# Node passes in rank order, with a pipeline of its own on each engine

## What is computed

```python
x = _layernorm(x + _L0_gnn_ref(x, edge_index, 12500, L0_gnn_W), axis=-1)
x = _layernorm(x + _L1_gnn_ref(x, src, dst, L1_gnn_W_n, L1_gnn_a_src, L1_gnn_a_dst, ...), axis=-1)
x = _layernorm(x + _L2_gnn_ref(x, edge_index, L2_gnn_W, L2_gnn_b), axis=-1)
x = _layernorm(x + _L3_gnn_ref(x, edge_index, edge_weight, L3_gnn_We1, ...), axis=-1)
```

## Time and profile before

| | us |
|---|---|
| median of 3 runs | 9929.16 |
| lowest, highest | 9925.69, 9943.68 |
| profiled execution, its own time | 9940.12 |
| its span | 9938.3 |

### The profile page before, as it was taken

One profiled execution on the slowest core, in us unless ns is written; L12 is line 12 of the kernel. 1 busy time (PEld: TensorE's weight loads), 2 busy tenths in 40 slices (PEclk: granted clock), 3 DMA queues, 4 the chain that ended last, 5 costly groups with the idle time before them and its releaser, 6 DMA issues. The chain is left out here.

```text
span 9938.3 us, 113228 instructions
## 1 busy us (share of the span) xinstructions
PE 5334.2 (54%) x29001; PEld 4290.1 (43%) x29001; DVE 5628.4 (57%) x12677; ACT 1827.5 (18%) x6201; POOL 6156.5 (62%) x6454
## 2 busy tenths in 40 slices
PE   0255555555366666666664454454435666666653
PEld 0233444444255555555553333333334555555532
DVE  2467777775477777777332222222256777777745
ACT  0000000001155555555320000000021111111121
POOL 0777777771577777776007777777636777777700
PEclk9866666667688988888885555555567777777766
DMA  4222222221444444444111111111234444444411
GB/s 101 71 54 54 53 54 54 54 52 50 114 120 118 121 120 119 119 119 104 47 48 53 53 53 53 53 53 53 64 111 117 119 119 119 119 118 119 118 37 35
DMA packets 932390, 822.38 MB, mean 83 GB/s; under 512 B 370017, under 2 KB 776073, under 8 KB 931435
## 3 DMA queue, kind: packets, MB, share of 16 engines
q0 software_dynamic: 231344, 523.28, 19.6%
q1 hardware_dynamic: 700480, 292.47, 11.6%
HBM read 735.15 MB, written 79.95 MB: 82 GB/s over the span
## 5 line engine op out<-in xcount | busy, mean ns | idle before, releaser
L682 POOL DMA_INDIRECT rows_h<-t_d,idx x3126 | 2991.8, 957 | 1290.1 <-issue 920.2
L811 PE MATMUL pn_h<-S_h,rows_h 128*128 128x128 f32 x9378 | 1817.7, 339 | 702.5 <-DVE lo_h L1004 459.1
L422 POOL DMA_INDIRECT rows_sum<-t_d,idx x1563 | 1478.2, 946 | 992.1 <-ACTq L359 515.9
L811 PEld LDWEIGHTS pn_h<-S_h,rows_h 128*128 128x128 f32 x9378 | 1559.3, 234 | 1019.8 <-issue 976.9
L422 POOL DMA_INDIRECT rows_mlp<-t_d,idx x1563 | 1482.2, 948 | 486.7 <-issue 476.4
L461 PE MATMUL pn_sum<-S_sum,rows_sum 128*128 128x128 f32 x3126 | 806.8, 440 | 970.2 <-DMA rows_sum<-t_d,idx 970.2
L461 PEld LDWEIGHTS pn_sum<-S_sum,rows_sum 128*128 128x128 f32 x3126 | 694.5, 327 | 1236.9 <-issue 1236.6
L720 ACT ACTIVATE rows_h<-rows_h,wc_h 128x64 f32<-128x64 f32 x4688 | 1133.8, 333 | 9.8
L529 DVE TENSOR_TENSOR acc<-acc,pn_sum 128x512 f32 x391 | 269.1, 688 | 1441.6 <-PE pn_sum L461 1441.4
L446 PE MATMUL pre_mlp<-dw_mlp,ST_mlp 128*128 128x128 f32 x3126 | 585.2, 346 | 764.8 <-DVE ST_mlp L56 764.1
L446 PEld LDWEIGHTS pre_mlp<-dw_mlp,ST_mlp 128*128 128x128 f32 x3126 | 502.6, 244 | 841.0 <-issue 789.2
(11 more groups left out here) (262 smaller groups left out, 7359.8 us busy)
## 6 DMA issues: line engine op xcount, KB each, us to landing
dw_mlp<-bd_d SPq DMA_DIRECT2D x1563, 64.0 KB
rows_h<-t_d,idx POOLq DMA_INDIRECT x3126, 2.5
n_xi<-x_d SPq DMA_DIRECT2D x56, 448.0 KB, 6.3
lrb_h<-lrrow_d SPq DMA_DIRECT2D x98, 256.0 KB
lrb_mlp<-lrrow_d SPq DMA_DIRECT2D x98, 256.0 KB, 3.5
dw_h<-sd_d SPq DMA_DIRECT2D x1563, 3.0 KB
rows_sum<-t_d,idx POOLq DMA_INDIRECT x1563
rows_mlp<-t_d,idx POOLq DMA_INDIRECT x1563
```

The costliest lines, as they stand in the source:

```text
L422: e.indirect_dma_start(rows[:, g % NR, j, :], None, table, bass.IndirectOffsetOnAxis(ap=idx[:, b, t:t + 1].bitcast(I32), axis=0)).then_inc ...
L682: e.indirect_dma_start(rows[:, g % NR, j, :], None, table, bass.IndirectOffsetOnAxis(ap=idx[:, b16, t:t + 1].bitcast(I32), axis=0)).then_i ...
L811: last = e.matmul(pn[g % 2][:, k, bass.ds(r0, P)], rows[:, g % NR, j, k * P:(k + 1) * P], S[:, g % NS, j, :], start=False, stop=last_tile)
```

## The change

Only node pass 0 still takes node order in. It scatters the normalized rows by rank to `xp_d`: 136 columns, which are x, the target scores in 6, the degree and the node number. The table `t1_d` gets one more column, the rank of its node, and the edge pass of layer 1 copies it from the gathered rows over `idx`, batch by batch. So later tables and gathers are in rank order, and `node1`, `node2` and `node3` read the accumulator `big` as it lies. `big[:, 0]` holds x between passes; GpSimd clears `big[:, 1]` during node passes 1 and 2, in the place of a clearing at the start of the edge passes. `node3` sends each tile of the result to its nodes with an indirect DMA. The one-hot matrix, the windows, the copy and the turn of the window, and x_d go from passes 1 to 3; the scatter goes from pass 2; passes 1 and 2 store plainly.

Each node function is written out as straight-line programs over 25 units of four tiles (the last has two), one for each engine, with a semaphore for each hand-over. Centring and scaling of a layer norm become one ScalarE activation for each tile (scale and bias by partition). In passes 2 and 3, which need gelu and square root, units go in chunks of 6, 6, 6, 4, 2 and 1, and the square roots of a chunk are taken together. Pass 3 multiplies We2 and Wu1's lower half once ahead of the loop (`V`) and so does one 512-column product less for each unit. Biases are added in passes 2 and 3 by a matmul over one row.

In the edge pass of layer 1, local ranks and `dw` come in blocks of 8 tiles, not 16; `dw` reads 24 of the 544 bytes of a row of `xp_d`, and `ex` waits for its own block, not for all 32 tiles of the batch. In the setup, 100 clearing DMAs of `bd_d` and one of `sd_d` become two small ones, and the store of `x_d` goes.

```diff
-W0, W1 = F + 1, H * DH + H
...
+W0, W1, XR = F + 1, H * DH + H + 1, F + 8
...
-                for k in range(DRANKS // P):
-                    e.dma_start(bd_d[k * P:(k + 1) * P, :], zero[:, 0:F]).then_inc(s_st, 16)
-                e.dma_start(sd_d.rearrange("(p k) h -> p (k h)", p=P),
-                            zero[:, 0:DRANKS // P * 3 * H // 2].bitcast(BF16)).then_inc(s_st, 16)
+                for table, w in ((bd_d, F), (xp_d, XR)):
+                    e.dma_start(table[NP:DRANKS, :].rearrange("(p k) f -> p (k f)", p=P), zero[:, 0:2 * w]).then_inc(s_st, 16)
...
-                e.dma_start(x_d.rearrange("(t p) f -> p t f", p=P), xs[:, :, 0:F]).then_inc(s_o, 16)
...
-            e.memset(acc[:, :, :], 0.0)
...
-                        m = (b * TB + k) // NB
-                        many = min(NB, have - k)
+                    for k in range(0, have, LB):
+                        m = (b * TB + k) // LB
+                        many = min(LB, have - k)
                         if m >= 2:
-                            e.wait_ge(s_st, (m - 1) * NB // 4)
-                        e.dma_start(lrb[:, m % 2, :], d["lrrow"][m:m + 1, :].broadcast_to([P, EB])).then_inc(s_lrb[m % 2], 16)
+                            e.wait_ge(s_st, (m - 1) * LB // 4)
+                        e.dma_start(lrb[:, m % 2, :], d["lrrow"].rearrange("(o b) e -> o (b e)", o=1)[:, m * LB * P:(m + 1) * LB * P]
...
-                        r0 = load_values(nc, SP, regs[BASE:BASE + 1, m * NB:m * NB + many], N)
+                        r0 = load_values(nc, SP, regs[BASE:BASE + 1, m * LB:m * LB + many], N)
                         for t in range(many):
-                            e.dma_start(dw[:, b % 2, k + t, :], d["sd"][bass.ds(r0[t], P), :]).then_inc(s_dw[b % 2], 16)
+                            e.dma_start(dw[:, b % 2, k + t, :], d["xp"][bass.ds(r0[t], P), F:F + 3 * H // 2]).then_inc(s_dw[m % 4], 16)
...
-                if g % GB == 0:
-                    if b > 0:
-                        e.wait_ge(s_chain, at(b - 1, "score"))
-                    e.wait_ge(s_dw[b % 2], 16 * sum(fetched[k] for k in range(b % 2, b + 1, 2)))
+                if g % GB == 0 and b > 0:
+                    e.wait_ge(s_chain, at(b - 1, "score"))
+                m = 4 * g // LB
+                if 4 * g % LB == 0:
+                    e.wait_ge(s_dw[m % 4], 16 * sum(min(LB, TILES - k * LB) for k in range(m % 4, m + 1, 4)))
...
+                        at0 = b * TB
+                        e.tensor_copy(idx[:, :, :].rearrange("p b t -> p (b t)")[:, at0:at0 + 4 * ng].bitcast(I32)
+                                      .rearrange("p (g t) -> p g t", t=4), rows[:, u:u + ng, :, W1 - 1])
                         e.wait_ge(s_ex, min(GR, (b + 1) * GB))
```

More of the change, by code:

```diff
@@ L1597, in node_pass @@
[L1597 to L1617 removed]
+            return ctx.enter_context(nc.semaphore(f"n0_{name}"))
@@ L1653, in _ @@
         @block.tensor
         def _(e):
[L1655 to L1663 removed]
+            e.wait_ge(s_w, 64)
+            for h in range(H):
+                for k in range(2):
+                    last = e.matmul(psc[0][:, 0, k * H + h:k * H + h + 1], wnT[:, h, :], a2[:, k, h:h + 1], start=True, stop=True)
@@ new lines, in _, with turn_acc, pick @@
+            last.then_inc(s_v, 1)
+            def turn_acc(u):
+                n = unit(u)[1]
+                e.wait_ge(s_win, u + 1)
+                if u > 0:
+                    e.wait_ge(s_Ar, u)
+                for j in range(n):
+                    last = e.transpose(pa[:, j, :], win[u % 2][:, j, :], ident[:, :])
+                last.then_inc(s_A, 1)
+            def pick(u):
+                n = unit(u)[1]
+                e.wait_ge(s_Ar, u + 1)
+                e.wait_ge(s_Es, u + 1)
+                if u > 0:
+                    e.wait_ge(s_y, u)
+                for j in range(n):
+                    last = e.matmul(pe[:, j, :], Es[u % 2][:, j, :], Ar[u % 2][:, j, :], start=True, stop=True)
+                last.then_inc(s_E, 1)
@@ new lines, in turn, with table @@
+            def turn(u):
+                n = unit(u)[1]
+                e.wait_ge(s_n, u + 1)
+                if u > 0:
+                    e.wait_ge(s_xT, u)
+                for j in range(n):
+                    last = e.transpose(pt[:, j, :], xs[u % 3][:, j, 0:F], ident[:, :])
+                last.then_inc(s_T, 1)
+            def table(u):
+                n = unit(u)[1]
+                e.wait_ge(s_xT, u + 1)
+                if u == 0:
+                    e.wait_ge(s_vs, 1)
+                else:
+                    e.wait_ge(s_tab, u)
+                if u >= 2:
+                    e.wait_ge(s_row, u - 1)
+                for j in range(n):
+                    last = e.matmul(ph[:, j // 2, j % 2, :], xT[u % 2][:, j, :], wn[:, :, :].rearrange("p h d -> p (h d)"),
+                                    start=True, stop=True)
+                last.then_inc(s_H, 1)
+                for j in range(n):
+                    last = e.matmul(psc[u % 2][:, j, :], xT[u % 2][:, j, :], vs[:, :], start=True, stop=True)
+                last.then_inc(s_S, 1)
@@ new lines, in normal, with hide @@
+            def normal(u):
+                t, n = unit(u)
+                e.wait_ge(s_rs, u + 1)
+                for j in range(n):
+                    last = e.activation(big[:, 0, (t + j) * P:(t + j + 1) * P], y[u % 2][:, j, :], ACT.Identity,
+                                        scale=rs[u % 2][:, j, :], bias=nm[u % 2][:, j, :])
+                last.then_inc(s_n, 1)
+            def hide(u):
+                n = unit(u)[1] * P
+                e.wait_ge(s_H, u + 1)
+                if u >= 2:
+                    e.wait_ge(s_O, u - 1)
+                for j in range(2):
+                    last = e.activation(hid[u % 2][:, j, 0:n], ph[u % 2][:, j, 0:n], ACT.Relu, bias=b1[:, j:j + 1])
+                last.then_inc(s_hid, 1)
@@ new lines, in turned @@
+            def turned(u):
+                n = unit(u)[1]
+                e.wait_ge(s_T, u + 1)
+                if u >= 2:
+                    e.wait_ge(s_G, u - 1)
+                e.copy(xT[u % 2][:, 0:n, :], pt[:, 0:n, :]).then_inc(s_xT, 1)
+            positive(0)
+            e.wait_ge(s_dn, 16)
+            e.activation(root[:, :], dn[:, :, 0], ACT.Sqrt, bias=c["ones"][:, 0:1]).then_inc(s_sq, 1)
+            for i in range(UNITS + 3):
+                if i + 1 < UNITS:
+                    positive(i + 1)
+                if 0 <= i - 2 < UNITS:
+                    normal(i - 2)
+                if i < UNITS:
+                    hide(i)
+                if 0 <= i - 2 < UNITS:
+                    turned(i - 2)
+                if 0 <= i - 1 < UNITS:
+                    deviate(i - 1)
```

1255 lines of the change are left out of this document (731 added, 524 removed).

## The result

| | before | after |
|---|---|---|
| median us | 9927.78 (4 runs) | 9308.01 (4 runs) |
| lowest to highest | 9925.69 to 9943.68 | 9301.27 to 9322.9 |
| span of the profiled execution | 9938.3 | 9299.4 |

The ratio is 0.9375, 95% interval 0.9358 to 0.9391: 620 us less, where 828 were forecast. The time lies inside the range.

A forecast was written before the change was run, and what follows sets the result against it. Edge passes were taken as bound by GpSimd's gathers, node passes by hand-overs between engines. Savings of 240 + 130 + 140 + 225 + 65 + 28 = 828 us, and 11 more, off 9940 gave 9100 us, range 8980 to 9340.

The forecast's parts named there:

- The bound before, edge passes by gathers: Edge passes: each lasts as long as its 1,563 gathers, 1.25 us each, 1955 us; no other engine can shorten it.
- Pass 1, -240: Node pass 1: PE sets the pace at 7.3 us a unit, 216 us in all, saving 240 us.
- Pass 3, -225: Node pass 3: 98 new GpSimd scatters start near 95 us and set the end near 238, saving 225 us.
- Setup, -28: Setup: less clearing and no `x_d` store save 28 us.
- edge pass 1, -65: Edge pass 1: `ex` no longer waits for the whole batch; three quarters of 89 us, 65, saved.
- Pass 2, -140: Node pass 2: 4.6 us a unit with PE at full clock, 190 us in all, saving 140 us.
- rival A: Node passes: PE stays at half clock and sets the pace; total near 9350 us, chance 0.12.
- Pass 0, -130: Node pass 0: 6.2 us a unit, 203 us with rank map, start and drain, saving 130 us.
- Rival C: Passes 0 and 3: scatters slow to 1.9 us each beside a busy VectorE; total 9190 us, chance 0.1.
- Rival E: Edge pass 1: strided `dw` reads make SyncE's issues longer, so the kernel gets slower, near 10,300 us; chance 0.04.
- Rival D: Edge pass 1 gives nothing, since `ex` waits for the score chain; total 9165 us, chance 0.2.
- Rival B: Node passes: hand-overs cost 2 us more for each of 100 units, +200; total 9300 us, chance 0.15.

The follow-up runs named there:

- e7: Kernel before, with edge pass 1's expansion waiting only for its own block of 16 tiles: gathers span 1985.7 us for 2043.4, kernel 9866.2 us.
- e8: Changed kernel; pass 2 with products before x transposes, bias on VectorE, idle products in first chunk; four scatter buffers in pass 0: 9071.04 us, ratio 0.9134.
- e10: Changed kernel with four scatter buffers instead of three in node pass 0, nothing else: gap 283.4 us for 340.4, kernel 9248.78 us.
- e3: Changed kernel with node pass 2's bias added by VectorE instead of PE matmuls, on a disturbed chip: gap 246.9 us, control 373.1.

## Why the prediction was right, and where not

- **The bound before, edge passes by gathers: right.** Their spans moved by 4 to 5 us, and what was to be won lay in the node passes, the setup and one wait. For edge pass 1 the 1955 us of 1,563 gathers were a little short: it took 1989.1, against the sign "within 10 us of its gathers". By the windows a gather there kept GpSimd busy for 0.966 us (1509.62/1562), and for 0.943 in the sum pass (1473.96/1563).
- **Pass 1, -240, measured -265: right in the mechanism, with some luck in the price.** I took PE as the pace with 6.3 of 7.3 us; the trace has 6.55 us a unit with PE busy 50.0 of 50 us at clock 1.00. The 5.6 that busy time times mean clock gave was too low; the addition for short pieces and the margin of 1 us covered it.
- **Pass 3, -225, measured -221: GpSimd's sends set its end, as forecast; that the start fitted to 0.5 us is luck.** The first send was forecast at 95 us from the start; it came at 9147.51 - 9052 = 95.5:

```profile
9147.51 1.02 POOL L1998 DMA_INDIRECT out<-n_z,gout  x1 [102.84 <-ACT n_z L2097]
...
9288.82 0.98 POOL L1998 DMA_INDIRECT out<-n_z,gout  x1 [0.30 <-DMA out<-n_z,gout]
```

GpSimd waited 118.9 us in all for the results, 102.84 of them before the first send, and the sends took 141.3 us, for 134. In that start PE was the pace, not VectorE as forecast; it had no idle time in a unit of the first chunk, at full clock:

```profile
9068.16 0.60 PE L2018 MATMUL n_pt<-ident,big 128*128 128x128 f32 x4
...
9069.56 1.12 PE L2031 MATMUL n_pu<-n_dg,n_v 1*128 1x512 f32 x2
9070.61 1.12 PE L2033 MATMUL n_pu<-n_xT,n_wu 128*128 128x512 f32 x2
...
9073.71 0.60 PE L2018 MATMUL n_pt<-ident,big 128*128 128x128 f32 x4
```

That is 5.55 us (9068.16 to 9073.71) for PE's 3.6 of the forecast, and it fell on the 5.5 that I had for the unit. The two chunks ahead of the first send took about 79 us for 63, against a start and boundaries that were shorter; and the forecast's own terms, 14, 30, 33 and two boundaries, come to 85 and not 95 if a boundary is the 4 us of pass 2. In the other runs on undisturbed chips the first send came 2 us earlier to 14 us later.
- **Setup, -28, measured -28.6, and edge pass 1, -65, measured -54: right.** The three quarters that I took were about the size; e7 shows the wait as the only cause. (2.0 us in each of the pass's 49 batches are 98 us, not the 89 of the forecast.)
- **Pass 2, -140, measured +24: wrong, and this is the step that failed.** "3.4 a unit, and with two bias matmuls about 3.2 at full clock" scaled PE's busy time by the mean granted clock of the window, 0.64. But that mean runs over the idle time too, and the busy time lay more at full clock than the idle time. The products of L1505 before ran nearly all at full clock (45.6 us for 392, 0.116 each); of the 113 us in which PE was busy, 67 lay at full clock and 46 at half. At full clock all of it is then 67 + 46/2 = 90 us, an estimate, and without L1481 some 67, 2.7 a unit and not 2.2. The bias rows I took at 0.76 us each before scaling, both together 1.0 at full clock; but a float32 matmul stands in the trace as two instructions, and one bias row of 512 columns is both of them. PE's busy time in the unit above is 9.97 us at half clock, so about 5.0 at full, for the 3.2 of the forecast; 2.1 of them are bias. Second, I took full clock for granted there, though rival A had the other price. Rival A came true in this pass alone ("if PE stays at 0.5 in a node pass" was among the signs of being wrong), and with 9.97 us of PE a unit, not its 6.5, since its price for half clock rested on the same scaling. Third, I read ScalarE's and VectorE's programs for their sums, not for their order beside PE's; the 3.5 us of waiting in each unit were in the order of the three programs and could have been read there.
- With the order turned and the bias off PE, e8 runs at 4.58 us a unit and a gap of 186 us: the pace of 4.6 that the forecast had, and about the 190 us. The size was reachable, not reached; the changed kernel with its two bias matmuls would not have had that pace even at full clock, by the 5.0 estimated above.
- **Pass 0, -130, measured -81: a term of the sum mis-sized.** Pace 6.2 was forecast; 196.5 us over 25 units is 7.9. The scatters themselves were cheap, 0.969 us, below both rows that I had. What was missing is the time for which a buffer is held: filled at step i+2, scattered after step i+4, and landed 2.4 us behind. I had counted engines and no buffers. With four, e10 gives 142.7 us, 5.7 a unit. The clock, 0.73 in this pass, was below the 0.8 that I expected, and PE's price of 3.7 was low here as well: in the middle of e8's pass 0, at full clock, a unit takes 5.29 us (2394.98 to 2400.27), of which PE is idle 0.29.
- **Rival C (scatters slowed by VectorE): false.** 969 ns in pass 0, 1018 in pass 3, for 1016 and 1063 before, beside a VectorE that is busy 40% and 53% of the time. VectorE never got to the 85% of the forecast, so what the forecast draws there from the Trainium skill had no full test.
- **Rival E (`dw` reads): false.** SyncE's 1,563 issues have a median of 333 ns before and after.
- **Rival D (edge pass 1 gives nothing): false**, -54.
- **Rival B (hand-overs)** holds in part: 1 us was enough in passes 1 and 3, 3.5 us came in pass 2 and the ring in pass 0.
- **Luck in the total.** The time lies inside the range because the range was wide: two of the four node passes miss their terms by 49 and 164 us, pass 1 gives 25 back, and PE's price was too low in all four. The clock was to be above 0.8 in the node passes and VectorE busy over 70% of pass 1; measured were 0.73, 0.93, 0.51 and 0.76, and 60% (113.94 of 191).

## What to carry to other kernels

Price PE work at full clock from a burst that ran at full clock, not from busy time times the mean clock; then work out the pass at half clock too, and ask which stretches of waiting will decide between them. When a program is cut into pipelines of several engines, walk once around the loop of waits in program order, and count for each buffer how many steps pass from its filling to its release: the miss of pass 0 and much of that of pass 2 lay there, and no engine's sum shows them. A float32 matmul with one row on the contraction side was no cheaper on PE than a full one.

## What the runs showed of the hardware

- A float32 matmul over one row with 512 columns took 2.07 us at half clock, as much as two of 256 columns over 128 rows (2.08); at full clock it took 1.12 us in pass 3, as much as one of 512 columns over 128 rows (L2031 and L2033).
- Adding work made the pass faster: with idle products in PE's waits 288 us, without them 365, at 0.78 to 0.92 of full clock for 0.51.
- The share of busy time alone does not tell the clock: PE was busy 246 of 359 us in pass 2 at 0.51 and 51 of 100 us in e3's pass 2 at 0.73. At half clock the same work counts about twice in busy time: the four products of a unit took 4.16 us, and 1.99 at full clock.
- One stretch of 10.87 us of waiting took PE from full clock (0.66 us for four transposes) to half (1.11 us), and behind it, with the 3.5 us of waiting in each unit, the clock came back for moments only (0.50 to 0.53 over the windows).
- An indirect scatter costs GpSimd nearly the same for rows of 24, 512 and 544 bytes: 1016, 1018 and 969 ns.
